# A mixture-of-experts kernel on one core: the row scatters left over from the mixer stage follow one behind each tile's result scatter

## The reference, cut to what matters

```
h = layernorm(x) * (1 + ca) + sa
x = x + ga * mixer(h)                    # silu(h @ Win), a scan with decay 0.9, @ Wout
h = layernorm(x) * (1 + cb) + sb
p = softmax(h @ Wr + br); probs, idx = top_k(p, 2)
for each expert e of a token:
    a = layernorm(relu(h @ W1[e] + b1[e])) * g1[e] + be1[e]     # 128 -> 512
    y = layernorm(relu(a @ W2[e] + b2[e])) * g2[e] + be2[e]     # 512 -> 128
x = x + gb * sum(gate * y)
```

## Time and profile before

| | us |
|---|---|
| runs | 566.27, 567.21, 570.75 |
| span of the profiled execution | 569.8 |
| its share with TensorE busy | 512.4 (90%) |
| DVE, ACT, POOL busy | 456.1, 413.5, 358.7 |
| result scatters on POOL (135, lines of two forms) | 119.8 + 15.9 |
| row scatters on POOL (128) | 123.3 |

### The profile page before, as it was taken

The page is one execution under the profiler, slowest core; times in us unless marked ns, Lnnn a source line. Parts: engine busy times, 40 slices in busy tenths (PEclk is TensorE's granted clock), DMA queues, the critical chain, the costliest instruction groups (busy, mean ns, idle before and its releaser), DMA issues.

```text
span 569.8 us, 14516 instructions
## 1 busy us (share of the span) xinstructions
PE 512.4 (90%) x3101; PEld 398.9 (70%) x3101; DVE 456.1 (80%) x2217; ACT 413.5 (73%) x1148; POOL 358.7 (63%) x483
## 2 busy tenths in 40 slices
PE   7889899988875479899989899999999999999996
PEld 7456454444444368677877778999999999999972
DVE  6778788878775348767777778999999999999993
ACT  5677778767563336576776768988888888888883
POOL 1004565646566556666666666788888788888871
PEclk9999999999987579899999999999999999999999
DMA  6950111237111134455575455666666756765855
GB/s 179 308 159 29 38 49 37 83 84 122 43 42 49 42 81 116 128 129 153 167 147 140 121 147 159 184 179 178 177 177 194 196 160 177 198 195 160 225 161 147
DMA packets 79785, 77.76 MB, mean 136 GB/s; under 512 B 11151, under 2 KB 72746, under 8 KB 79703
## 3 DMA queue, kind: packets, MB, share of 16 engines
q1 hardware_dynamic: 71286, 59.92, 41.2%
q0 software_dynamic: 8416, 16.93, 8.4%
HBM read 54.65 MB, written 22.59 MB: 136 GB/s over the span
## 4 chain that ended last, share of the span: by engine, by line
PE 64%; DVE 17%; ACT 8%; issue 6%; another core or an unknown queue 5%; POOL 0%; DVEq 0%; POOLq 0%
PE bank L1679 20%; PE bank L1574 9%; PE bank L1569 6%; PE bank L1566 6%; PE bank L1567 5%; PE bank L1568 5%; PE bank L1558 2%; PE bank L1511 2%; ACT n L755 2%; DVE scan L1161 2%; DVE st L1219 2%; PE bank L1544 1%; DVE st L1086 1%; ACT h2T L770 1%
## 5 line engine op out<-in xcount | busy, mean ns | idle before, releaser
L646 POOL DMA_INDIRECT expert_rows<-rows_ring,slot x128 | 123.3, 963 | 122.1 <-issue 74.6
L1679 PE MATMUL bank<-W,h2T 128*128 x1080 | 147.1, 280 | 8.8 <-ACT h2T L770 4.4
L1679 PEld LDWEIGHTS bank<-W,h2T 128*128 128x128 f32 x1080 | 134.1, 195 | 12.4 <-issue 12.2
L672 POOL DMA_INDIRECT expert_results<-y,target x119 | 119.8, 1006 | 36.3 <-issue 35.8
L766 ACT ACTIVATE h1T<-bank 128x512 f32<-128x512 f32 x135 | 80.4, 595 | 50.4 <-PE bank L1569 36.9
L1144 DVE BATCH_NORM_STATS2 stf<-h1T 128x6 f32<-128x512 f32 x135 | 90.9, 673 | 0.0
L770 ACT ACTIVATE h2T<-bank 128x512 f32<-128x512 f32 x135 | 79.4, 588 | 15.1 <-remote 13.8
L1574 PE MATMUL bank<-ident_wr,h1T 128*128 128x128 f32 x540 | 82.1, 275 | 2.8 <-ACT h1T L766 1.7
L1574 PEld LDWEIGHTS bank<-ident_wr,h1T 128*128 128x128 f32 x540 | 67.6, 142 | 23.2 <-issue 3.5
L1566 PE MATMUL bank<-b_parts,onesr 128*128 x135 | 66.0, 489 | 5.7 <-issue 3.1
L1363 DVE SCALAR_TENSOR_TENSOR wmod<-bank,rse,shifts 128x128 f32<-128x128 f32 x119 | 40.9, 344 | 27.7 <-remote 14.2
(11 more groups left out here) (241 smaller groups left out, 1071.6 us busy)
## 6 DMA issues: line engine op xcount, KB each, us to landing
shifts<-expert_shifts SPq DMA_DIRECT2D x119, 192.0 KB
hrow<-expert_rows SPq DMA_DIRECT2D x135, 65.0 KB
xi<-expert_results SPq DMA_DIRECT2D x12, 512.0 KB
out_x<-X SPq DMA_DIRECT2D x15, 256.0 KB
X<-in_L_attn_x SPq DMA_DIRECT2D x7, 512.0 KB, 7.3
W1lo<-in_L_ffn_W SPq DMA_DIRECT2D x4, 512.0 KB, 6.8
expert_rows<-rows_ring,slot POOLq DMA_INDIRECT x128
expert_results<-y,target POOLq DMA_INDIRECT x119
```

What stands on the lines that cost most here:

```text
L646: nc.gpsimd.indirect_dma_start(out=rows_d, out_offset=bass.IndirectOffsetOnAxis(ap=slot[q][:, n // TOPK, n % TOPK:n % TOPK + 1], axis=0), ...
L672: nc.gpsimd.indirect_dma_start(out=results_d, out_offset=bass.IndirectOffsetOnAxis(ap=target[i % TARGETS][:], axis=0), in_=y[k], in_offset ...
L1679: ins = mm(acc, rT[q][:, ch * P:(ch + 1) * P], W2[:, bass.ds(e2 * CF + ch, 1), :], start=(ch == 0), stop=(ch == CF - 1))
```

## The change

POOL issues no row scatter between the last batch's two and the first tile's addition: the loop of seven times two goes, with its 14 waits. In the loop over tiles the condition on odd i goes: a row scatter follows each tile's result scatter (tile 0 has only the scatter of rows) until all are sent. Nothing else is changed; the order in which rows are sent is the same.

```
-            FILLING = 7
...
-            for i in range(FILLING):
-                pool.wait_ge(r_ready, i + 1)
-                pool.nop(nofuse=True)
-                store_next(1)
-                pool.wait_ge(mve_ready, i + 1)
-                pool.nop(nofuse=True)
-                store_next(1)
...
             for i in range(LAST_SHIFTED):
...
                 add_shift(i)
                 if i > 0:
                     store_results(i - 1)
-                if i % 2 == 1 and sent[0] < B * J * TOPK:
+                if sent[0] < B * J * TOPK:
                     store_next(1)
```

## The result

| | runs | median us | lowest to highest |
|---|---|---|---|
| before | 4 | 566.74 | 565.88 to 570.75 |
| changed | 4 | 579.77 | 577.51 to 580.33 |

The ratio is 1.0213 (95% interval 1.0175 to 1.025). The medians differ by 13.0 us, where the forecast was 5.0 slower. The two profiled executions are the slowest of each four, 570.75 and 580.33 us, so their spans (569.8 and 578.3) show 8.5 us of the 13.0.

The account below looks back on a forecast made before the run. TensorE, busy for 90% of the span, and what keeps it idle were taken to set the end. The terms -6.9 + 16.4 - 4.5 gave +5.0 us, so 572 us, with 8 in 10 for 556 to 584.

Parts of the forecast that it names:

- B: Tiles 7 to 43: delay grows with the run of scatters, from 3.42 us per step; 576 to 588 us; chance 0.34.
- The mechanism named: Ahead of tile 55: beside row scatters, TensorE's finished work is made known 2 to 3 us late.
- The 14 scatters that go: Tiles 4 to 7: without the run of row scatters, three steps fall from 14.0 to 7.1 us, -6.9 us.
- The 22 of odd tiles become 36: Tiles 7 to 43: one row scatter per tile at 1.02 us makes the step 3.39 us, +16.4 us.
- Tiles 43 to 55: Without row scatters, these 12 steps take 28.5 us in place of 33.0, -4.5 us.
- The base: Whole kernel: profiled span 569.8 us, 0.5% over the median of 567.2; the difference was carried to the median.
- POOL's queue: Tiles 0 to 35: the row scatter ahead of every next addition delays nothing that matters; priced at nothing.
- SP waiting at line 515: Sign in tiles 0 to 35: such a wait would mean the wrong mechanism was named; no size given.
- the cover: At 3.39 us per step POOL needs 2.91 and keeps up; without that, tile 40 to 50 about 1 us late.
- Rival A: Tiles 7 to 43: delays do not grow, POOL's 2.91 us is the step; -12.2 us, 555 us; chance 0.27.

Follow-up runs that it names:

- g3: The changed kernel with all 128 row scatters issued in the mixer stage, eight a batch, on a late chip: 589.28 us, ratio 1.0298.
- e4: The kernel of g3 on a prompt chip, with 36 row scatters issued again at tiles 0 to 35 into a table that nothing reads: 553.18 us.
- h1: The kernel of e4 once more, unedited (520 bytes a row), on a prompt chip: 553.7 us.
- h3: The kernel of e4 with 8 bytes a row in the 36 scatters issued again, on a prompt chip: 555.29 us.
- i2: The kernel of e4 with 512 bytes a row at a pitch of 512 in the scatters issued again, on a prompt chip: 552.38 us.
- f6: The kernel before, unedited, profiled on a prompt chip: median 520.15 us over 15 runs.
- g2: The kernel before, unedited, profiled on a late chip: median 571.77 us over 13 runs.

## Why the prediction was wrong

It forecast no clear change, 0.8% slower; 2.1% was measured. The time is inside the range, and the case that came true is B. The mechanism named, row scatters that come with late marks, is the right one on late chips; sizes were off.

*The 14 scatters that go.* Right, to 0.1 us in the first pair (-6.9), -7.3 on the second late chip (14.4 to 7.1 us for three steps). The reason given, that the delay comes from the run of row scatters, is backed by g3, which has the same loss in the same tiles beside the end of its own run, and by the changed kernel, which has neither. On a prompt chip this term is nothing: tiles 4 to 7 take 7.1 us with the 14 scatters and without.

*The 22 of odd tiles become 36, +16.4.* **This step failed, by its size, and with it the next one:** from tile 7 to tile 55 the forecast was +11.9 us, and +16.2 and +21.3 were measured on the two late chips. The price of 1.02 us per row scatter was taken from a cycle in which they are sparse, and carried to a stretch with one in each tile. Over the plain 2.371 us, the 20 row scatters issued between tiles 7 and 43 cost 20.4 us before (1.02 each), and the 36 of the changed kernel 38.4 (1.07); on the second late chip it is 21 for 19.5 (0.93) and 36 for 44.7 (1.24). So the step per tile is 3.44 and 3.61 us where I had 3.39, both beyond the 3.42 from which B decides, and the term is +18.0 and +25.3. The kernels' medians differ by 13.0 and 12.0 us there. B's reason (the price grows with the density) agrees with these, weakly in the first pair (1.02 to 1.07), and isn't shown beyond them; that "only an empty POOL lets TensorE's signals through" is contradicted by g3's tile stage, where POOL issues a result scatter per tile and no mark is late.

*Tiles 43 to 55, -4.5.* -1.8 in the first pair, as tiles 44 and 51 still took 4.5 and 3.0 us; -4.0 on the second late chip. The last row scatter is issued at 331.7 us and tile 44's hidden layer comes at 336.6, so the stretch was not free of their consequences: 2.7 us too much credit, more than the 1.6 us of the step above in this pair.

*The base.* The profiled execution of before was the slowest of its runs, 4.0 us over the four runs' median, and the changed kernel's 0.6 over its own. A sum of differences within one slow execution is the smaller for it. These 3.4 us, 1.6 and 2.7 from the two terms, less 0.7 ahead of tile 4, and 1.1 us that lie outside the spans (the run's time is 1.0 us over its span before, 2.1 after) make up the 8.0 us between +5.0 and +13.0, but for rounding.

*POOL's queue, at nothing.* Right on late chips: the changed kernel has no wait at line 515 between 160 and 350 us, since steps of 3.44 us leave POOL no lag. On prompt chips it is the whole effect, and SP waiting at line 515 is the sign that the prediction gave for a wrong mechanism. I had named the cover ("at 3.39 us per step POOL needs 2.91 and keeps up") and priced the case without it at a lag of about 1 us. The right price was in the rows: POOL 2.93 (2.91 in the rows) against TensorE 2.37 over 36 tiles is 20 us less what the slots absorb, and it was paid as 12.7 us in one step. I hadn't asked where a lag that the slots hide is paid back: where their number halves, at tile 40.

*Rival A* (POOL's own 2.91 us is the step) did not come true on any chip with the changed kernel; TensorE went at that pace only in e4 and the kernels made from it (h1 to h3, i2), from about tile 22 on (2.93 us per tile). The Trainium skill's rule that it leaned on ("SBUF — State Buffer", the part on who interferes with whom: TensorE and ACT never wait on anyone) speaks of ports, and no run shows a port conflict of TensorE or ACT; what doesn't hold on late chips is the step from that rule to "a scatter could not slow them". What was late is the mark behind TensorE's work; the Trainium skill's "Perfetto Trace Analysis" (the section on the Tensor Engine's instruction) says that the profiler's end is an estimate and that the semaphore update is pushed only once PSUM has acknowledged the bytes, and then propagates. In the rows above, 2.25 us lie between that end and ACT's start on a late chip and 0.30 on a prompt one. Since DVE's marks come late as well, TensorE's own way of ending can't be the whole of it.

## What to carry to other kernels

Where an engine falls behind and buffers hide it, look for the place at which the number of buffers shrinks: the lag is paid there in one piece (12.7 us here), and a lighter rate (two in three tiles instead of each) all but avoids it. A price per instruction taken from a stretch where such instructions are sparse can be too low for a stretch where they are dense: 1.02 and 0.93 us became 1.07 and 1.24. Before a change is priced by one profile, the same kernel is best profiled on a second chip: here it differed by 9%, with another bound.

## What was not expected of the hardware

The same kernel took 520 us on some chips and 567 to 572 on others, at nearly the same mean granted clock (0.986 in f6, 0.964 in g2). On the latter, row scatters (indirect DMAs of 128 rows issued by POOL, 0.96 us each) come with late completion marks of TensorE, and in the mixer stage of DVE too. In the median TensorE's late marks are 1.5 to 2.0 us late in five of the six profiles, and 3.2 us in g3's. Result scatters (1.00 us each, also 128 rows, but with a bounds check, another source and another table) come with none. Both instructions last as long on POOL on either kind of chip (0.96 and 0.99 us in the medians of f6 and g2). How many bytes a row has makes no difference to POOL's time: the instruction takes 0.96 us with 8, 512 and 520 bytes, and 36 scatters of 8 bytes a row (h3) cost what 36 of 520 do (h1), within 0.3%.
